# Another order for VectorE's and ScalarE's share of an edge turn, and seven rounds of twelve turns written out

## What is computed

```python
def _prop_once(node_states, f_idx, t_idx, edge_features, w1, b1, w2, b2, w3, b3):
    edge_inputs = concatenate([node_states[f_idx], node_states[t_idx], edge_features], axis=1)
    edge_states = _mlp(edge_inputs, w1, b1, w2, b2, w3, b3)     # relu, relu, linear: 384 -> 256 -> 256 -> 128
    return segment_sum(edge_states, t_idx, num_segments=3125)
agg = _prop_once(x, edge_attr, src, dst, ...) + _prop_once(x, edge_attr, dst, src, ...)
# then three GRU cells, x = layernorm(x + s3)
# then three rounds of X = relu(((1 + eps) * X + segment_sum(X[src], dst)) @ W1 + b1) @ W2 + b2, x = layernorm(x + X)
```

## Time and profile before

| | us |
|---|---|
| median of 3 runs (2472.25 to 2475.75) | 2475.32 |
| the profiled execution | 2480.43 |
| its span | 2478.3 |
| PE busy in the span | 2295.4 (93%) |
| DVE busy | 1753.3 (71%) |
| POOL busy | 1413.0 (57%) |
| ACT busy | 1211.6 (49%) |

### The profile page before, as it was taken

One profiled execution on the slowest core, in us unless ns is written; L12 is line 12 of the kernel. 1 busy time (PEld: TensorE's weight loads), 2 busy tenths in 40 slices (PEclk: granted clock), 3 DMA queues, 4 the chain that ended last, 5 costly groups with the idle time before them and its releaser, 6 DMA issues. The chain is left out here.

```text
span 2478.3 us, 42263 instructions
## 1 busy us (share of the span) xinstructions
PE 2295.4 (93%) x12547; PEld 1887.8 (76%) x12547; DVE 1753.3 (71%) x4057; ACT 1211.6 (49%) x2106; POOL 1413.0 (57%) x846
## 2 busy tenths in 40 slices
PE   5999999999999999999999999999999959799997
PEld 3777787877877887887787787877878845488886
DVE  7877787877887887887787787887878746711114
ACT  4555555555555555555555555555555504311112
POOL 2676577767767776776777677767767510000000
PEclk9999999999999999999999999999999969899998
DMA  4456555345555354555355554455554371195963
GB/s 156 79 106 114 99 93 97 82 90 92 104 95 93 79 98 91 98 103 93 72 104 93 97 103 88 79 104 91 98 101 86 51 191 56 71 365 233 369 265 150
DMA packets 232387, 292.97 MB, mean 118 GB/s; under 512 B 126015, under 2 KB 189861, under 8 KB 223799
## 3 DMA queue, kind: packets, MB, share of 16 engines
q1 hardware_dynamic: 158756, 237.04, 34.3%
q0 software_dynamic: 73216, 54.58, 17.5%
q10 hardware_dynamic: 272, 0.05, 0.0%
HBM read 218.51 MB, written 73.08 MB: 118 GB/s over the span
## 5 line engine op out<-in xcount | busy, mean ns | idle before, releaser
L470 POOL DMA_INDIRECT sums<-outb,target x416 | 703.4, 1691 | 430.1 <-ACT outb L633 222.9
L463 POOL DMA_INDIRECT xg<-in_x,gidx x416 | 704.9, 1694 | 161.0 <-issue 140.3
L615 ACT ACTIVATE h<-ebank,b2c 128x512 f32<-128x512 f32 x416 | 287.3, 691 | 376.6 <-PE ebank L1217 319.1
L1229 PEld LDWEIGHTS ebank<-w3t,h 128*128 128x128 f32 x3328 | 387.4, 192 | 8.3 <-issue 0.3
L1229 PE MATMUL ebank<-w3t,h 128*128 128x128 f32 x3328 | 388.2, 275 | 0.2 <-ACT h L615 0.2
L1217 PE MATMUL ebank<-h1h,w2h 128*128 128x512 f32 x832 | 367.2, 441 | 3.9 <-DVE h1l L846 3.9
L1217 PE MATMUL ebank<-h1h,w2l 128*128 128x512 f32 x832 | 330.5, 397 | 0.0
L1217 PE MATMUL ebank<-h1l,w2h 128*128 128x512 f32 x832 | 328.0, 394 | 0.0
L609 ACT ACTIVATE h1h<-hpre 128x512 fp32r<-128x512 f32 x416 | 237.7, 622 | 152.8 <-issue 89.9
L846 DVE SCALAR_TENSOR_TENSOR h1l<-hpre,h1h 128x512 fp32r<-128x512 f32 x416 | 259.0, 684 | 0.0
L1203 PE MATMUL ebank<-sdh,w1h 128*128 128x512 f32 x624 | 244.2, 391 | 2.1 <-DVE sdl L867 1.4
(11 more groups left out here) (268 smaller groups left out, 4090.5 us busy)
## 6 DMA issues: line engine op xcount, KB each, us to landing
ring<-adj SPq DMA_DIRECT2D x54, 1568.0 KB, 8.0
rowb<-along SPq DMA_DIRECT2D x104, 512.0 KB
adj<-band SPq DMA_DIRECT2D x25, 1500.0 KB
ef<-in_edge_attr SPq DMA_DIRECT2D x103, 256.0 KB
stay<-adj SPq DMA_DIRECT2D x6, 1568.0 KB, 14.5
xg<-in_x,gidx POOLq DMA_INDIRECT x416
sums<-outb,target POOLq DMA_INDIRECT x416
sums<-band SPq DMA_DIRECT2D x2, 1664.0 KB
```

Of the source, the lines that this page charges most:

```text
L463: pool.indirect_dma_start(out=to, out_offset=None, in_=a["x"], in_offset=bass.IndirectOffsetOnAxis(ap=ids, axis=0)).then_inc(s_x[par], 16)
L470: pool.indirect_dma_start(out=tables[k % 2], out_offset=bass.IndirectOffsetOnAxis(ap=target[par][:, 1, k:k + 1], axis=0), in_=outb[par][:, ...
L615: nc.scalar.activation(h2[:, way, f, :], bank[6 + f][:, :], ACT.Relu, bias=b2c[:, f:f + 1]).then_inc(s_h2, 1)
L1229: last = nc.tensor.matmul(bank[6 + way][:, t * P:(t + 1) * P], h2[:, way, k, t * P:(t + 1) * P], w3t[:, k, :], start=not bias and k == 0, ...
```

## The change

The waits and the order of the instructions change on DVE and ACT; on PE only the order in which the first layer takes its inputs (s before the features, to fit the new order of their low parts). No instruction with data is added or taken away.

- DVE's turn: `nodes` and `compare` stand ahead of `sums`; the two `count_pairs` stand together, ahead of `lower_parts`; `lower_parts` makes the low parts of s and d first and of the features second; `window` stands behind `pair_hot`.
- `ways` and ACT's `first` are interleaved: one half's sum and difference, its first low part, then the other half. The semaphore `s_hp` counts each way by itself (4 a turn in place of 2).
- ACT's turn: `xs_out` ahead of `second(g, 0)`, `upper_sd` ahead of `second(g, 1)`, `upper_e` behind it.
- The seven rounds are written out on DVE and ACT. The loop's index becomes a constant.

```diff
                 def first(g):
...
+                    shared(0)
                     act.wait_ge(s_l2, g * 4)
+                    hidden(0, 0)
+                    shared(1)
+                    hidden(0, 1)
+                    hidden(1, 0)
+                    hidden(1, 1)
...
                 def turn(g, par, turns, ahead=2, early=False, cleared=None):
+                    if win and ahead:
+                        xs_out(g + 1)
                     second(g, 0)
                     if ahead:
-                        if win:
-                            xs_out(g + 1)
-                        else:
-                            upper_sd(g + 1)
+                        upper_sd(g + 1)
                     second(g, 1)
                     if ahead:
                         upper_e(g + 1)
-                        if win:
-                            upper_sd(g + 1)
...
-                    with act.Fori(0, ROUNDS) as m:
+                    for m in range(ROUNDS):
...
             def ways(g):
+                both(0)
+                rest(0, 0)
+                both(1)
+                rest(0, 1)
+                rest(1, 0)
+                rest(1, 1)
...
                     if ahead:
+                        nodes(g + 1, 1 - par, early=early == 2)
+                        compare(g + 1, 1 - par, turns + par)
                         sums(g + 1)
...
-                    if not begin:
-                        count_pairs(g, 0)
-                    if ahead:
+                    count_pairs(g, 0)
+                    count_pairs(g, 1)
+                    if ahead and not begin:
                         lower_parts(g + 1)
...
-                    if ahead:
-                        compare(g + 1, 1 - par, turns + par)
                     if ahead == 2:
                         onehot(g + 2, par, turns + 1)
+                    if ahead:
+                        pair_hot(g + 1)
+                    if ahead == 2:
                         window(g + 2, par)
                     if ahead:
-                        pair_hot(g + 1)
                         ways(g + 1)
...
-                with dve.Fori(0, ROUNDS) as m:
+                for m in range(ROUNDS):
...
-                    pe.wait_ge(s_hp, g * HB)
+                    pe.wait_ge(s_hp, g * 4)
...
-                    for bk, signal, js in ((2, s_p, (2, 0)), (3, s_q, (1,))):
+                    for bk, signal, js in ((2, s_p, (0, 2)), (3, s_q, (1,))):
```

More of the change, by code:

```diff
@@ L600, in first, with shared @@
                 def first(g):
-                    for f in range(HB):
+                    def shared(f):
                         act.wait_ge(s_p, g * HB + (f + 1))
@@ L604, in first, with hidden @@
                                              bias=b1c[:, f:f + 1]).then_inc(s_pc, 1)
+                    def hidden(f, way):
+                        act.wait_ge(s_hp, g * 4 + (f * 2 + way + 1))
+                        nc.scalar.activation(h1h[:, way, f, :], hpre[:, f, way, :], ACT.Relu).then_inc(s_h1, 1)
+                    shared(0)
                     act.wait_ge(s_l2, g * 4)
-                    for f in range(HB):
-                        act.wait_ge(s_hp, g * HB + (f + 1))
-                        for way in range(2):
-                            nc.scalar.activation(h1h[:, way, f, :], hpre[:, f, way, :], ACT.Relu).then_inc(s_h1, 1)
+                    hidden(0, 0)
[3 more added lines that the diff above has]
+                    hidden(1, 1)
                 def second(g, n):
@@ L682, in program @@
                     xs_out(0)
+                    upper_sd(0)
                     upper_e(0)
-                    upper_sd(0)
                     upper(1, 1, 0)
@@ L836, in ways, with both, rest @@
             def ways(g):
[L837 removed]
+                def both(f):
                     dve.wait_ge(s_pc, g * HB + (f + 1))
                     dve.wait_ge(s_q, g * HB + (f + 1))
[L840 to L848 removed]
+                    for way, op in enumerate((ALU.add, ALU.subtract)):
+                        nc.vector.tensor_tensor(hpre[:, f, way, :], pb[:, f, :], bank[3 + 2 * f][:, :], op).then_inc(s_hp, 1)
+                def rest(f, way):
+                    dve.wait_ge(s_h1, g * 4 + (f * 2 + way + 1))
+                    nc.vector.scalar_tensor_tensor(
+                        out=h1l[:, way, f, :], in0=hpre[:, f, way, :], scalar=0.0,
+                        in1=h1h[:, way, f, :].bitcast(fp32), op0=ALU.max, op1=ALU.subtract).then_inc(s_h1l, 1)
+                both(0)
[4 more added lines that the diff above has]
+                rest(1, 1)
             def windowed():
```

28 lines of the change are left out of this document (7 added, 21 removed).

## The result

The changed kernel takes 2451.89 us (2444.41 to 2457.89, 6 runs) against 2474.73 us (2470.99 to 2483.47, 6 runs) of the kernel before on the same chip: ratio 0.990 [0.988, 0.992]. It is faster by 23 us, not by 99; the time lies 60 us above the forecast's own range (2366 to 2392) and 42 us above the end of the wider one (2410). Its profiled execution took 2451.4 us, 29.1 less than that of before.

The account below looks back on a forecast made before the run. PE bounds the kernel, losing 0.81 us a turn waiting for ACT's `es` because of DVE's order. The hundred turns save 97.5 us, the first two 2, together 99: 2480.4 to 2381.4, minus 5.1 to the median, 2376 us; range 2366 to 2392 (0.75).

Parts of the forecast that it names:

- the wider one: Whole kernel: the time was to lie between 2362 and 2410 us 8 times in 10.
- The floor of an ordinary turn, 17.56: PE: without the wait before L1277 an ordinary turn falls from 18.37 to 17.56 us, as in turn 101 to 102.
- The 0.73 us between the counts: DVE: the second count waits 0.73 us behind the first, new 104 times, but DVE has them to spare.
- The low parts: ACT and DVE: low parts of s and d at 7.3, features at 7.9; PE's new input order covered with 0.8 us to spare.
- `wrap` turns, 1.1 us left: Eight turns with `wrap` ahead of `ways`: PE's wait falls from 2.44 us to about 1.1 us each.
- `nodes` and `compare` into the wait, "They cost nothing": DVE's front: both fill the wait before `sums`, done at 1.9 of the turn, at no cost.
- a mild rival: POOL or loads: `rowb` asked for some 4 us sooner, beside the adds; turn ends at 18.1, 2430 us; chance 0.05.
- the two counts together: DVE: both counts follow the pair products, the first at 4.0, the second at 5.5 and done at 6.1 of the turn.
- Turn 8 and the clock, 7.4 us: Late scatter-add in turn 8 plus lower clock behind `wrap` turns: 7.4 of 18.4 us left, ends 3 and 21.
- The written-out rounds, 0: DVE and ACT: writing out the rounds is worth 0, range 0 to 0.1 us for each of 84 turns, either sign.
- the rival that POOL's gathers bind: POOL: gathers or adds stopped longer by DVE make POOL's turn 18.8 us, kernel slower, 2505 us at 19.0; chance 0.04.
- the sum's 1772.2: Hundred turns from 1 to 101: 1756.0 us of ordinary turns, plus 8 x 1.1 for `wrap`, plus 7.4: 1772.2 us, 97.5 less.

Follow-up runs that it names:

- n_late_eold: The changed kernel with the band write held until `hpre`, the ways not interleaved and the low parts edge part first again: 2370.93 us, ratio 0.955.
- h_late_ways_old: The changed kernel with the band write held until the first `hpre` and the two ways not interleaved: 2367.64 us, ratio 0.956.
- d_compare_early: The kernel before with only `nodes` and `compare` moved ahead of `sums`: 2411.03 us, ratio 0.974.
- m_compare_old: The changed kernel with `nodes` and `compare` put back where they were: 2437.66 us, ratio 0.982.
- a_write_late: The changed kernel with one more wait on SP, so the band write goes out only at the first `hpre`: 2373.37 us, ratio 0.958.
- p_early_unrolled_mid: The kernel before with `nodes` and `compare` ahead of `sums`, rounds written out, band write released by the first `colhot` group: 2452.36 us, ratio 0.989.
- i_late_loops: The changed kernel with the band write held until the first `hpre` and DVE's and ACT's seven rounds as loops again: 2390.08 us, ratio 0.964.

## Why the prediction was wrong, step by step

- *The floor of an ordinary turn, 17.56*: right, 17.53, and its steps with it. In the turn whose `total` is at 965.80 the second count is at 5.5 (summed: 5.5), the low parts end at 8.0 (7.9), `hpre` starts at 10.8 (10.8) and `es` at 14.7 (14.9).
- *The 0.73 us between the counts*: right, 0.74, and free. *The low parts*: free in ordinary turns; n_late_eold shows that their new order was not needed there and is worth 0.5 us in a `wrap` turn.
- *`wrap` turns, 1.1 us left*: PE's idle time is 0.63 to 0.73 us, and these turns take 18.3 to 18.5 us, 0.8 to 1.0 over an ordinary one. By h_late_ways_old this is the price of the interleaving.
- *`nodes` and `compare` into the wait, "They cost nothing"*: **this step failed.** On DVE it is true. But `compare` also releases `rowb` on SP, and the write of the band stands behind `rowb`. The prediction followed `rowb` alone ("asked for with `compare`'s earlier end, some 4 us sooner in the turn, beside the adds"), as a mild rival, and didn't go on to the next entry of the same queue, 1.5 MB, which overtook the fourth add. Nor did it ask, at *the two counts together*, what the earlier second count releases: the write. With the one move and not the other it goes out at 9.3 (d_compare_early), with the other and not the one at 10.4 (m_compare_old), and neither does harm. Together they have a price of 78 us, shown by a_write_late.
- *Turn 8 and the clock, 7.4 us*: the mechanism was read as a scatter-add "behind the first large writes", but the earlier trace rows don't show what stood ahead. SP's rows of before do: the loads for the later stages, then a write 8.3 us ahead of the next adds (200.68). Large transfers ahead of scatter-adds had thus made `target` late once in the profile before, and I priced it as a single event. The clock's part rose instead of falling, with the new gaps.

```profile
170.07 1.03 SPq L1486 DMA_DIRECT2D x<-in_x  x2
...
192.37 0.64 SPq L359 DMA_DIRECT2D adj<-band  x1
```

- *The written-out rounds, 0*: right in the order of before, wrong in the new one, where they give 17 to 18 us. "DVE and ACT have idle time in each turn that hides it" no longer holds with ACT's relu behind `upper_sd` and the low parts behind both counts. A DVE pause of 3.15 us is larger than any wait of the earlier trace rows. The Trainium skill (Runtime: NRT & Kernel Launch, Instruction fetch mechanics), which the prediction weighed and set aside, was the better guide in so far as these pauses stand at the loops' returns and are gone with the rounds written out; what DVE does in them no trace shows.
- *POOL*: the rival that POOL's gathers bind did not come. The gathers' mean fell from 1694 to 1084 ns. But its state seems to decide how the kernel bears the write, as far as the rows of p_early_unrolled_mid show it.

The forecast of 2376 us would have stood with the write late: 2373.4 us in a_write_late. That agreement is in part luck. The hundred turns take 1760.3 us there, 12 less than the sum's 1772.2, and the profiled execution 2371.4, 10 less than its 2381.4. The 5.1 us taken off for the step from the profiled execution to the median then made up for part of it, since here the median lies 2.0 us above. And the rounds had to be written out for it: with loops the same kernel takes 2390.1 us (i_late_loops), so a change whose worth was put at 0 carries 17 us.

## What to carry to other kernels

When an instruction moves, follow each semaphore that it signals to the queue that waits for it, and read on down that queue: what is issued behind the released entry moves as well. A large plain write and small indirect writes that someone waits for share the DMA engines, so the write needs a place of its own in the turn, behind this turn's and well ahead of the next; fix it with a wait of its own, not by what happens to stand before it in the queue. And a cost that is hidden now, like a loop's return, has to be priced again for the new order: look for who waits behind the engine that pauses.

## What the runs showed of the hardware, unexpected

- A small scatter-add that is issued just behind a 1.5 MB write lands 14.6 us behind it. In that time the DMA share is 0.76 or more in every microsecond (992 to 1008), and in the next one it is 0.05; that the add lands only when the write is through is read from this. With 0.72 MB in that place `target` waited at most 1.2 us.
- A write that is issued a little behind the add's start still goes with a late landing. With the write 0.4 us ahead, the fourth add landed 14.3 us after its start (993.02 to 1007.28); with the write 0.8 us behind it, 11.8 us (402.73 to 414.54, p_early_unrolled_mid). With 1.4 us it had landed within 10.5 us (331.02 to 341.48, d_compare_early), which is when `target` came. Whether it is late depends on the room, too: in p_early_unrolled_mid the add starts 3.3 us later in the turn. How sharp the edge is, the runs don't show.
- In most turns of the kernel before one gather takes 3.8 us, where it starts with DVE's run of `h1l`, `match` and `found` and ends with it; 3.19 us in p_early_unrolled_mid, where it starts 0.75 us into the run. It is not the start against the run that decides: in the kernel before the 32 gathers that start within 0.1 us of the run's start take 3.8 to 3.9 us too, and in h_late_ways_old, whose run is as long and as unbroken, nearly all that start beside it or inside it take 0.9 to 1.5 us. What decides stays open.
- DVE stood still for up to 3.15 us at a loop's return, 18.2 us in seven times, six of them 2.9 us or more (i_late_loops). With the rounds written out these pauses are gone.
